# Storing two of 32 tiles as 120 rows and 8 rows in a LoRA kernel

## The reference

```python
B_sel = B[adapter_ids]                              # 64 x 16 x 1024
A_sel = A[adapter_ids]                              # 64 x 1024 x 16
Bx = jnp.einsum('bni,bri->bnr', x, B_sel)
out = jnp.einsum('bnr,bor->bno', Bx, A_sel)
return x + out * SCALING                            # SCALING = 1
```

## Time and profile before

| | |
|---|---|
| median of 3 runs | 92.29 us (92.13 to 92.45) |
| the profiled execution, its time | 91.97 us |
| the profiled execution, its span | 90.2 us |
| busy in the span: PE, PEld, DVE, ACT, POOL | 81.0, 61.4, 59.2, 59.8, 62.9 us |
| bytes moved by DMA | 34.82 MB, mean 386 GB/s |

### The profile page before, as it was taken

The page is one execution under the profiler, slowest core; times in us unless marked ns, Lnnn a source line. Parts: engine busy times, 40 slices in busy tenths (PEclk is TensorE's granted clock), DMA queues, the critical chain, the costliest instruction groups (busy, mean ns, idle before and its releaser), DMA issues.

```text
span 90.2 us, 3586 instructions
## 1 busy us (share of the span) xinstructions
PE 81.0 (90%) x1451; PEld 61.4 (68%) x1451; DVE 59.2 (66%) x110; ACT 59.8 (66%) x155; POOL 62.9 (70%) x141
## 2 busy tenths in 40 slices
PE   3998989899999999999999999999999999989200
PEld 3996758678787868787878787786868687543000
DVE  0309965349595968687786859595959595999000
ACT  1339867968696969696969695959687777542200
POOL 6103991999999999979797979796979692900000
PEclk9999999999999999999999999999999999999855
DMA  2999999999999999999999999999999999998980
GB/s 19 324 411 414 407 412 409 405 416 412 391 411 411 409 409 409 400 421 411 421 416 414 418 427 398 421 412 418 416 412 416 425 402 420 418 372 327 409 345 35
DMA packets 9346, 34.82 MB, mean 386 GB/s; under 512 B 499, under 2 KB 1011, under 8 KB 9331
## 3 DMA queue, kind: packets, MB, share of 16 engines
q1 hardware_dynamic: 7600, 27.79, 77.2%
q10 hardware_dynamic: 1730, 6.82, 18.7%
HBM read 17.83 MB, written 16.78 MB: 384 GB/s over the span
## 4 chain that ended last, share of the span: by engine, by line
PE 76%; DMA 6%; ACT 4%; POOL 3%; issue 2%; DVE 2%; POOLq 0%
PE t_bank L255 31%; PE bx_bank L268 19%; PE y_banks L288 17%; DMA x_all<-in_A 6%; PE y_banks L316 2%; PE t_bank L320 2%; ACT x_t L378 2%; POOL a_duo L181 2%; POOL b_duo L188 1%; PE bx_bank L320 1%; DVE x_all L448 1%; DVE x_all L443 1%; ACT bx_parts L393 1%; PE bx_bank L316 1%; ACT x_all L366 1%
## 5 line engine op out<-in xcount | busy, mean ns | idle before, releaser
L468 DVE TENSOR_TENSOR x_all<-y_banks,x_all 128x1024 f32<-128x1024 f32 x29 | 35.5, 1224 | 14.5 <-PE y_banks L288 14.0
L378 ACT COPY x_t<-t_bank 128x512 f32<-128x512 f32 x64 | 34.4, 589 | 13.0 <-PE t_bank L255 12.4
L198 POOL CAST a_duo<-a_table 128x512 fp32r x64 | 36.6, 615 | 3.8 <-ACT a_table L383 2.0
L255 PE MATMUL t_bank<-ident,x_all 128*128 128x128 f32 x256 | 35.0, 280 | 0.7 <-ACT x_t L378 0.7
L255 PEld LDWEIGHTS t_bank<-ident,x_all 128*128 128x128 f32 x256 | 27.4, 141 | 8.0 <-issue 5.3
L188 POOL COPY b_duo<-b_table 128x256 f32 x64 | 22.9, 401 | 5.6 <-PE bx_bank L268 5.6
L268 PE MATMUL bx_bank<-x_t,b_duo 128*32 128x64 f32 x1024 | 20.7, 222 | 0.0
L268 PEld LDWEIGHTS bx_bank<-x_t,b_duo 128*32 128x32 f32 x1024 | 15.7, 109 | 5.5 <-issue 5.5
L288 PE MATMUL y_banks<-a_duo,bx_parts 64*128 64x512 f32 x112 | 16.7, 417 | 0.0
L459 DVE TENSOR_TENSOR bx_parts<-bx_bank,bx_parts 32x64 fp32r<-32x64 f32 x64 | 14.1, 220 | 2.7 <-ACT bx_parts L393 1.6
L393 ACT CAST bx_parts<-bx_bank 32x64 fp32r<-32x64 f32 x64 | 13.0, 204 | 1.9 <-PE bx_bank L268 1.3
(11 more groups left out here) (31 smaller groups left out, 22.8 us busy)
## 6 DMA issues: line engine op xcount, KB each, us to landing
x_all<-in_x SPq DMA_DIRECT2D x5, 2048.0 KB, 25.1
out_y<-x_all ACTq DMA_DIRECT2D x3, 2048.0 KB, 16.7
x_all<-in_x SPq DMA_DIRECT2D x4, 1024.0 KB, 13.9
out_y<-x_all SPq DMA_DIRECT2D x4, 1024.0 KB, 10.7
out_y<-x_all SPq DMA_DIRECT2D x8, 512.0 KB, 5.0
x_all<-in_x SPq DMA_DIRECT2D x4, 512.0 KB, 7.3
out_y<-x_all SPq DMA_DIRECT2D x1, 2048.0 KB, 15.2
x_all<-in_A SPq DMA_DIRECT2D x1, 512.0 KB, 5.3
```

Of the source, the lines that this page charges most:

```text
L198: last = nc.gpsimd.tensor_copy(a_duo[duo % 2][:, k, :], a_table[:, bass.ds(adapters[k] * BANK, BANK)])
L255: last = nc.tensor.transpose(t_bank[unit % 2][:, c * P:(c + 1) * P], x_all[:, 2 * duo + tile, at:at + P], ident[:, :])
L378: nc.scalar.copy(x_t[duo % 2][:, half * HALF:(half + 1) * HALF, tile, :], t_bank[unit % 2][:, :].rearrange("p (c n) -> p c n", c=HALF)).th ...
L468: nc.vector.tensor_tensor(here, product, here, ALU.add).then_inc(y_drained, 1)
```

## The change

The stores of tiles 24 and 25 are each issued as two transfers, of rows 0 to 119 and of rows 120 to 127 of the tile. The final wait counts two transfers more. The waits ahead of the stores stay as they are, and both parts of a tile stand behind the same one.

```diff
     STORES = [(12, 16)] + [(t, t + 2) for t in range(16, 24, 2)] + [(t, t + 1) for t in range(24, TILES)]
+    BY_FIFTEEN, MOST = (24, 25), 120
...
-                sp.dma_start(out_rows[:, first:end, :], x_all[:, first:end, :]).then_inc(stored, 16)
-            sp.wait_ge(stored, 16 * (len(STORES) + len(STORES_BY_ACT)))
+                if first in BY_FIFTEEN:
+                    for part in (slice(0, MOST), slice(MOST, P)):
+                        sp.dma_start(out_rows[part, first:end, :], x_all[part, first:end, :]).then_inc(stored, 16)
+                else:
+                    sp.dma_start(out_rows[:, first:end, :], x_all[:, first:end, :]).then_inc(stored, 16)
+            sp.wait_ge(stored, 16 * (len(STORES) + len(STORES_BY_ACT) + len(BY_FIFTEEN)))
```

## The result

The changed kernel is slower. Over 20 runs each, its median is 92.47 us and that of the kernel before 92.13 us; the ratio is 1.0040, with a 95% interval of 1.0028 to 1.0051. That is +0.37 us (0.26 to 0.47). I had forecast a gain of 0.4 us; what came is close to the first rival, "relief of the wrong engine", which stood at +0.32 us.

A forecast was written before the change was run, and what follows sets the result against it. The bound was one late DMA engine finishing the last stores. Issue cost 0 and relief of 0.5 to 0.2 us, taken as -0.4, gave 91.6 us on the profiled 91.97 and 91.9 on the median; range 91.65 to 92.7.

The forecast's parts named there:

- the first rival: Store tail: an early engine is spared and the last one gets two extra rows; +0.32 us, 92.6 us; chance 0.22.
- What bounds the kernel: Tail: the end waits for a single DMA engine, 1.65 us behind the bulk and 0.5 us behind the next.
- Issue: SP's queue: two new issues, 0.7 us together, lie in waits for VectorE; cost 0.
- Data: Stores of tiles 24 and 25: one engine spared 16 rows, 2.58 us; eight engines get 0.32 us more.
- Who gains: Tail: the spared engine is the last, so the second-latest ends the program; gain 0.5 us, or 0.2 with extra rows.
- no effect: Tail: last engine neither spared nor loaded, or rows spread over all 16; end stays, 92.3 us; chance 0.18.
- the case with it: Tail: last engine relieved, but the second-latest gets the extra rows; -0.2 us; chance 0.24.
- The twelve early engines hide 0.32 us: Before the tail: the extra 0.32 us on early engines fits in their 0.7 us of holes.
- The large piece runs slower: Stores of 120 rows: two engines may read the same SBUF part at once; about 93.5 us; chance 0.08.
- The second-latest as the bound: Tail: the second-latest engine, with its extra rows, ends the program; 92.1 us, the forecast's low end; chance 0.24.

The follow-up runs named there:

- the early pair: Kernel before, with tiles 16 and 17 stored as 112 rows each and their last 16 partitions in six small transfers: ratio 0.9991 (0.9966 to 1.0017).

## Why the prediction was wrong

*What bounds the kernel* was right: the end is one late DMA engine. It stands alone at the end of every tail shown but that of the early pair, and in the changed kernel its end did not follow a last store that was issued 0.7 us later.

*Issue*, costed at 0, was right, though one of the new issues took 1.21 us and not 0.34. SP has 15 issues in place of 13, and 112 and 16 rows gave 1.0005, with as many transfers as the change.

*Data* was right in its split, as the packet counts show. 120 rows spare one engine, 8 rows load eight, and a row costs 0.13 to 0.20 us on the late one: two rows 0.36 to 0.40 us, four rows 0.68, eight rows 1.07 to 1.37. The rule of the Trainium skill, "DMA: Bandwidth & Descriptors", section "Why a DMA increments its semaphore by 16 and not by 1" (the largest divisor up to 16, on the lowest-numbered engines) fits all of these: transfers of four and of five rows differ by one engine, and that engine decides. That they are the lowest-numbered ones is only consistent with the times, since the trace doesn't number the engines.

*Who gains* is the step that failed. I gave the case that the spared engine is the last one a chance of 0.52, with nothing in the rows that says which engine is last, as the text itself noted. By count alone it would be 1 in 16, or 1 in 4 if the spared engine were known to be one of the late four, and that the last one is among the eight that get extra rows 1 in 2. The first rival had 0.22 and should have led; only no effect, 7 in 16, comes near it. The weighing inside the forecast was turned round as well: of the 15 other engines 8 get the extra row, so the case with it, -0.2 us, had the larger chance. What the runs showed in its place: sparing one engine 16 rows moved the end by +0.12 us (-0.09 to +0.34), the last engine carried the small piece in the changed kernel's own packets, and small transfers alone cost +0.40 us. The first rival's price, +0.32 us, was right within the interval. With the spared engine not last, only the added rows are left of the change, and the late engine has no hole to put them in.

*The twelve early engines hide 0.32 us* was right for the two that were tried: eight extra rows on the first, or the first two, cost nothing that can be measured.

*The large piece runs slower*, the rival with 0.08: rows are slower there (375 GB/s for a full share in the changed kernel, 378 with the large pieces alone, 317 with 112 and 16 rows, 399 before), but at 375 to 378 GB/s it costs nothing that can be measured: the execution with the large pieces alone took 91.89 us.

*The second-latest as the bound* never came up, since the last engine was not relieved. Its rule (the Trainium skill, "DMA: Bandwidth & Descriptors", section "Latency and other measured facts", engines 7 and 15 usually slower) does not fit here: counted from 0 as there, the last engine is number 4 by the runs above. That section's own best guess ties the rule to transfers that GpSimd issues, and here SP and ScalarE issue all of them.

The range reached from 91.65 to 92.7 us and held the 92.47, but only as the outcome of a rival; the sign was wrong.

Still open: why that engine is late, whether it is the same one on every chip, and whether taking rows from it helps while the last store is issued as late as it is.

## What to carry to other kernels

When the tail of a store-bound kernel shows one or a few DMA engines busy, find out which they are before moving rows among them: extra transfers of n rows, for rising n, show it in a few runs. By the rule above, a split that doesn't divide by 16 loads the low engines, and if one of these is the last, every extra row is paid in full. When such probes disagree with each other, compare the GB/s with the share of busy engines first. The packet count of a queue tells how many engines a transfer used, and completions at the right distance before the end tell whether the last engine was one of them.

## What the runs showed of the hardware that was not expected

Four engines that read neighbouring partitions in the same transfers were slowed: eight transfers of partitions 124 to 127 cost +1.07 us, and of partitions 0, 4, 8 and 12 +0.29, with 300 against 398 GB/s for a full share from 80 to 82 us. The two ran on different chips and wrote to different rows of `spare`, so the partitions are the likely cause and not a separated one; with seven rows, neighbours and spread cost the same (+1.30 and +1.33). The Trainium skill, "SBUF — State Buffer", section "Door 1", says that four neighbouring partitions lie on one port; the numbers with four rows agree. Transfers of 120 and of 112 rows have slower rows than transfers of 128 (375 to 378, once 317, against 399 GB/s for a full share); why, no run here shows. And a late DMA engine is not the accident of one execution: medians over several executions pay for rows on one of the first eight on three chips (+1.37 on one, +1.27 on the second, +1.30 on the third). What makes it late no run here shows.
